# Gated cross block on one core: h of the last tiles turned by a transposing DMA instead of by TensorE

## The chip, the core and the metric

The kernel runs on one core of a Trainium2 chip. A core has four compute engines, each with its own instruction stream: TensorE (PE, matrix products and transposes into PSUM), VectorE (DVE), ScalarE (ACT) and GpSimd (POOL), and a fifth, SyncE (SP), which here only issues DMA transfers. They are kept in step by semaphores. The metric is the device time of one execution in microseconds (us), and the median of several runs is compared.

## The reference

The inputs are x (4 x 512 x 512), a context (4 x 512 x 256), two gates and weights. A selective scan (Mamba) over the context gives a branch that is gated by the layer-normed x and added to x; then a feed-forward block with quantised activations and ternary weights is added. Only the second half matters to this change:

```python
def _act_quant(x):
    scale = 127.0 / jnp.clip(jnp.max(jnp.abs(x), axis=-1, keepdims=True), EPS)
    return jnp.round(jnp.clip(x * scale, -128.0, 127.0)) / scale      # forward value
def _bitlinear(x, w):
    return jnp.einsum('bsi,oi->bso', _act_quant(_rmsnorm(x)), _weight_quant(w))
gate = jax.nn.silu(_bitlinear(x, w_gate))          # 512 -> 2048
up = _bitlinear(x, w_up)                           # 512 -> 2048
return _bitlinear(gate * up, w_down)               # h = gate * up, 2048 -> 512
x = x + tanh(g_xattn) * mamba(ctx, layernorm(x));  x = x + tanh(g_ffn) * ffn(layernorm(x))
```

## The kernel before, in words

The 2048 rows of x (4 batches of 512) are 16 tiles of 128 rows. The scan half works in 16 units s of 128 channels, and from unit 4 on the feed-forward part of tile s - 4 runs between the instructions of unit s. After the last unit (s = 15) the feed-forward parts of tiles 12 to 15 are left, with the end of tile 11 and the down projection of tile 10. This last stretch, from about 550 us on, is where the change acts.

What a tile t needs there, with the names and lines of the code:

- `xq_late` / `xq_transpose` (L546): four TensorE transposes of the quantised x, copied by ScalarE to `xqT` (`copy_xqT`, L1052).
- `late_gate` and `late_up` (L552): for each of four chunks c of 512 columns, four matmuls for gate and four for up.
- `gate_silu` (L1060, ScalarE) and `times_up` (L1406, VectorE) make one chunk of h, 128 x 512 floats. h of a tile is 128 x 2048.
- `squares` (L1066, ScalarE), `h_max` (L1410, VectorE), `h_rstd` (L831, GpSimd, 128 x 1) and `h_scales` (L1419 to L1424, VectorE) give the quantising factor.
- `scale_h` (L1088, ScalarE), twice, each half of h: times the factor, plus MAGIC = 1.5 * 2^23, which rounds to an integer.
- `hq_transpose` (L583, TensorE): 16 transposes of 128 x 128, four into each of four PSUM fillings, in two groups of eight; `copy_hqT` (L1093, ScalarE), four times, each taking MAGIC off and writing bf16 to `hqT`.
- `down` (L596, TensorE): 16 matmuls with the ternary down weights into `pT`; `output` (L1430, VectorE) scales it, adds x, and `store` (L322, SP) writes it out.

Each engine's order is written out by hand. In the tail's iteration of tile t TensorE does gate and up of chunk 0, then the down projection of tile t - 2, then gate and up of chunks 1, 2 and 3, with the x transposes of tile t + 1 and the h transposes of tile t - 1 among them. ScalarE does four Silus, with `scale_h(t - 1, 0)` behind the second and `scale_h(t - 1, 1)` behind the third. In the iteration of tile 15 both scalings stand ahead of the second Silu. `down(t - 2)` for t = 13, 14, 15 belongs to tiles 11, 12, 13, and the down of tile 14 stands at the end of the iteration of tile 15. Tile 15 itself is quantised in quarters by VectorE (L1555) and transposed and projected in quarters (L769, L1279, L620). `hqT`, `xqT`, `xn` and `o_buf` have two buffers each, as has h in the tail (`h_main`, `h_late`).

## Time and profile before

| | us |
|---|---|
| median of 3 runs | 621.03 (620.51 to 621.07) |
| span of the profiled execution, first to last instruction | 617.3 |
| PE busy | 520.0 (84%) |
| DVE busy | 557.0 (90%) |
| ACT busy | 519.0 (84%) |
| POOL busy | 508.1 (82%) |

For the profiled execution itself only the span is given, no whole time; the span lies 3.7 us under the median of the runs. The shares are means over the whole program. In the page's 40 slices POOL is at 9 tenths until slice 35 and at 3, 1, 0, 0, 0 after it, PE at 9, 8, 9, 9, 9, 6 in the last six. So a change in the tail is to be read in rows of the tail. The granted clock of TensorE (PEclk) is 0.9 or more there; 1.00 is 2.4 GHz and 0.50 is 1.2 GHz.

### The profile page before, as it was taken

The page shows a single profiled execution, that of the slowest core. Times are in us where ns is not written, and L with a number is a line of the kernel's source. Part 1 is how long each engine was busy: PE and PEld are TensorE (multiplying, and loading weights), DVE is VectorE, ACT ScalarE, POOL GpSimd, SP SyncE. Part 2 cuts the span into 40 slices and gives each one's busy share as a digit, 9 for nine tenths or more (in the row PEclk, how much of TensorE's full clock was granted, in tenths as well). Part 3 has the DMA queues.
Part 4 walks back from the last instruction along what each step waited for, and adds up shares of the span by engine and source line. Part 5 has one row for each costly group of instructions (what it writes and reads, how often), then busy time and mean ns, then how long its engine had stood idle before and what let it go on. Part 6 is the DMA issues. An engine that isn't in the chain of part 4 may idle for free. (4 is left out here: it accounts for less than half of the span.)

```text
span 617.3 us, 9751 instructions
## 1 busy us (share of the span) xinstructions
PE 520.0 (84%) x3254; PEld 363.1 (59%) x3254; DVE 557.0 (90%) x766; ACT 519.0 (84%) x796; POOL 508.1 (82%) x286
## 2 busy tenths in 40 slices
PE   6999666757776888999879989998799898999996
PEld 2443355646664767676747666666467666655553
DVE  2899979999999899999899999998999999987564
ACT  4869788985998899899798999997988988768884
POOL 2568799999999899999999999999999999931000
PEclk9999768989699999999999999999999999999999
DMA  9992941620751010117501111175111110000001
GB/s 286 401 414 88 354 156 34 245 80 1 271 206 52 0 53 2 35 35 277 188 31 35 36 35 35 35 266 195 35 35 36 35 36 18 2 18 18 18 19 51
DMA packets 30420, 64.25 MB, mean 104 GB/s; under 512 B 3729, under 2 KB 11921, under 8 KB 27554
## 3 DMA queue, kind: packets, MB, share of 16 engines
q1 hardware_dynamic: 30370, 63.63, 29.1%
q8 instruction: 26, 0.43, 0.3%
q14 instruction: 24, 0.20, 0.1%
HBM read 55.49 MB, written 8.13 MB: 103 GB/s over the span
## 5 line engine op out<-in xcount | busy, mean ns | idle before, releaser
L850 POOL TENSOR_TENSOR area_s<-area_s,b_bc 128x1024 f32<-128x1024 f32 x117 | 275.0, 2363 | 13.8 <-DVE u_all L1454 9.2
L483 PE MATMUL pY<-ident,area_s 128*128 128x128 f32 x532 | 87.6, 290 | 56.6 <-DVE area_s L1462 56.6
L552 PE MATMUL pG<-wq_gu,area_f 128*128 128x512 fp8e4 x448 | 107.9, 379 | 4.0 <-ACT area_f L1052 2.9
L1454 DVE TENSOR_TENSOR_SCAN area_s<-pA,area_s 128x512 f32<-128x512 f32 x88 | 105.2, 1207 | 5.1 <-ACT pA L1107 4.4
L483 PEld LDWEIGHTS pY<-ident,area_s 128*128 128x128 f32 x532 | 61.6, 146 | 78.0 <-DVE area_s L1462 70.5
L1107 ACT ACTIVATE pA<-dt_all,a_neg 128x512 f32<-128x512 f32 x145 | 97.7, 682 | 10.7 <-DVE area_s L1454 5.9
L842 POOL TENSOR_TENSOR u_all<-u_all 128x1024 f32<-128x1024 f32 x44 | 103.9, 2361 | 0.2 <-DMA u_all<-bc_rows 0.2
L1462 DVE TENSOR_TENSOR area_s<-area_s,pC 128x512 f32<-128x512 f32 x133 | 87.9, 664 | 0.8 <-DVE area_s L1454 0.5
L477 PE MATMUL pC<-ident,xdT 128*128 128x128 f32 x532 | 83.2, 283 | 3.6 <-DVE area_s L1462 2.3
L477 PEld LDWEIGHTS pC<-ident,xdT 128*128 128x128 f32 x532 | 64.3, 143 | 8.9 <-DVE area_s L1462 7.4
L552 PEld LDWEIGHTS pG<-wq_gu,area_f 128*128 128x128 bf16 x448 | 41.7, 98 | 47.1 <-ACT area_f L1052 3.9
L596 PE MATMUL pT<-wq_dn,area_f 128*128 128x512 fp8e4 x240 | 57.5, 379 | 0.0
L483 PE MATMUL pY<-ident,u_all 128*128 128x128 f32 x352 | 48.7, 284 | 2.0 <-POOL u_all L842 2.0
L831 POOL TENSOR_TENSOR sm<-sm,neg_half 128x1 f32<-128x1 f32 x16 | 8.8, 552 | 44.9 <-ACT sm L1070 33.7
L483 PEld LDWEIGHTS pY<-ident,u_all 128*128 128x128 f32 x352 | 42.2, 147 | 5.3 <-POOL u_all L842 2.4
L1406 DVE TENSOR_TENSOR area_f<-area_f,pG 128x512 f32<-128x512 f32 x52 | 34.6, 678 | 8.3 <-PE pG L552 6.3
L1107 ACT ACTIVATE pC<-dt_all,a_neg 128x512 f32<-128x512 f32 x57 | 38.9, 683 | 3.4 <-DVE u_all L1454 2.4
L1454 DVE TENSOR_TENSOR_SCAN u_all<-pA,area_s 128x512 f32<-128x512 f32 x33 | 39.6, 1212 | 0.1
L1060 ACT ACTIVATE area_f<-pG,sm 128x512 f32<-128x512 f32 x52 | 34.4, 685 | 4.3 <-PE pG L552 3.3
L583 PE MATMUL pG<-ident,area_f 128*128 128x128 f32 x176 | 24.0, 278 | 15.9 <-ACT area_f L1093 13.1
L795 POOL TENSOR_TENSOR area_s<-area_s 128x511 f32<-128x511 f32 x16 | 20.0, 1269 | 20.0 <-DVE area_s L1293 20.0
L1454 DVE TENSOR_TENSOR_SCAN area_s<-pC,area_s 128x512 f32<-128x512 f32 x29 | 35.0, 1207 | 1.4 <-ACT pC L1107 1.4
(211 smaller groups left out, 1143.9 us busy)
## 6 DMA issues: line engine op xcount, KB each, us to landing
b_bc<-bc_rows SPq DMA_DIRECT2D x14, 1024.0 KB, 6.5
area_s<-x SPq DMA_DIRECT2D x32, 256.0 KB, 2.9
u_all<-bc_rows SPq DMA_DIRECT2D x14, 512.0 KB, 5.9
b_bc<-w_gate SPq DMA_DIRECT2D x1, 4096.0 KB, 14.5
dt_all<-x SPq DMA_DIRECT2D x1, 4096.0 KB, 24.8
area_f<-w_up SPq DMA_DIRECT2D x1, 4096.0 KB, 34.2
area_f<-w_down SPq DMA_DIRECT2D x1, 4096.0 KB, 14.4
out<-area_f SPq DMA_DIRECT2D x16, 256.0 KB, 2.1
```

Of the source, the lines that this page charges most:

```text
L477: mm = pe.transpose(c_bank(s, m)[:, k * P:(k + 1) * P], xdT[:, s // NT, k, NS + n:NS + n + 1].to_broadcast([P, P]), ident[:, :])
L483: mm = pe.matmul(pY[:, k * P:(k + 1) * P], src[:, k * P:(k + 1) * P], ident[:, :], is_transpose=True, start=(first and k == 0), stop=(last ...
L552: mm = pe.matmul(bank, xqT[t % 2][:, k, :], wq_gu[:, k, m, c * GW:(c + 1) * GW], start=(k == 0), stop=(k == NT - 1))
L583: mm = pe.transpose(banks[r % 2][:, k * P:(k + 1) * P], h_of(t)[:, (4 * r + k) * P:(4 * r + k + 1) * P], ident[:, :])
L596: mm = pe.matmul(pT[:, :], hqT[t % 2][:, k, :], wq_dn[:, k, :], start=(k == 0), stop=(k == FK - 1))
L842: gp.tensor_tensor(hp[j], hp[j], c_bc[j], ALU.mult).then_inc(S["s_pmul"], 1)
L850: gp.tensor_tensor(db[c % NDB], du[s % 2].rearrange("p (a l) -> p a l", a=1).to_broadcast([P, CH, L]), b_bc[:, CH * c:CH * c + CH, :], ALU ...
L1060: act.activation(h_of(t)[:, c * GW:(c + 1) * GW], bank, ACT.Silu, scale=col(CS[t % 2])).then_inc(S["f_silu"], 1)
L1107: act.activation(exp_bank(s, n), dt_all[:, s, :], ACT.Exp, scale=a_neg[:, s % NT, n:n + 1]).then_inc(S["s_exp"], 1)
L1406: dve.tensor_tensor(chunk, chunk, bank, ALU.mult).then_inc(S["f_h"], 1)
L1454: dve.tensor_tensor_scan(h, at, dbu, 0.0, ALU.mult, ALU.add).then_inc(S["s_scan"], 1)
L1462: dve.tensor_tensor(p_st[i % NH], h_st[i % NH], c_bank(s, m), ALU.mult).then_inc(S["s_mul"], 1)
```

## The change

For tiles 11 to 14 (`DMA_FROM` = 11) `hq_transpose` and `copy_hqT` are gone. In their place GpSimd takes MAGIC off each half of the scaled h and writes bf16 into `hb`, two new views of 128 x 2048 bf16 in space of `u_all` that the scan no longer uses (`h_whole`, semaphore `f_hb`); then SP issues one transposing DMA from `hb` to `hqT` (`turn_h`, semaphore `f_hqD`); then `down` waits for `f_hqD`. A Silu that writes over an h buffer now waits for GpSimd's passes of the tile before last, where it waited for TensorE's transposes. Tile 15 is done as before. The stores of tiles 11, 12 and 13 stand behind the next tile's `turn_h` on SP.

```diff
--- before.py
+++ after.py
@@ -42,6 +42,8 @@
 DPARTS = -(-FK // DK)
 HR = FK // 4
 
+DMA_FROM = UNITS - NT - 1
+
 
 def pooled(s):
 
@@ -108,7 +110,7 @@
     d_xz0 d_xz1 d_xr0 d_xr1 d_bbc0 d_bbc1 d_bbc2 d_bbc3 d_c0 d_c1 d_c2 d_c3 d_u0 d_u1 d_out0 d_out1
     s_exp s_dbu s_scan s_mul s_pmul s_pytr s_cb s_ytr s_du s_skip s_skd s_dup s_duT s_diag s_dbp s_amul s_aytr d_ca s_sz s_szp s_szT s_y s_x1
     f_bn f_sum f_dev f_ve f_rr f_xn f_xs f_e f_xm f_xqp f_xqT f_gate f_silu f_up f_h f_sq f_mh f_rh f_hs f_hm
-    f_hqp f_hqT f_dn f_o e_y e_x1 e_sq e_max e_ss""".split()
+    f_hqp f_hqT f_hb f_hqD f_dn f_o e_y e_x1 e_sq e_max e_ss""".split()
 
 
 def past(eng, sem, value):
@@ -213,6 +215,8 @@
 
         z_buf = [zn, zt]
 
+        hb = [u_all[:, 2 + 2 * i:4 + 2 * i, :].rearrange("p n l -> p (n l)").bitcast(BF16) for i in range(2)]
+
         pA = ps("pA", [P, 2, 512])
         pC = ps("pC", [P, 2, 512])
         pY = ps("pY", [P, 512])
@@ -386,8 +390,21 @@
                     load_c_alone(s // NT)
                 if s >= 7:
                     store(s - 7)
-            for t in range(UNITS - 7, UNITS):
-                store(t)
+            def turn_h(t):
+
+                past(sp, S["f_dn"], t - 1)
+                past(sp, S["f_hqD"], 16 * (t - DMA_FROM))
+                sp.wait_ge(S["f_hb"], 2 * (t - DMA_FROM) + 2)
+                sp.dma_start_transpose(hqT[t % 2], hb[t % 2]).then_inc(S["f_hqD"], 16)
+
+            store(UNITS - 7)
+            store(UNITS - 6)
+            for t in range(DMA_FROM, UNITS - 1):
+                turn_h(t)
+                if t > DMA_FROM:
+                    store(t - 1)
+            store(UNITS - 2)
+            store(UNITS - 1)
             sp.wait_ge(S["d_out0"], 16 * UNITS // 2)
             sp.wait_ge(S["d_out1"], 16 * UNITS // 2)
 
@@ -585,7 +602,10 @@
 
             def down(t, part, z_done):
                 if part == 0:
-                    pe.wait_ge(S["f_hqT"], HR * t + HR)
+                    if t < DMA_FROM:
+                        pe.wait_ge(S["f_hqT"], HR * t + HR)
+                    else:
+                        pe.wait_ge(S["f_hqD"], 16 * (t - DMA_FROM) + 16)
                     past(pe, S["f_o"], t)
 
                     if z_done < UNITS:
@@ -615,7 +635,7 @@
                         keep_on(s)
 
             def down_quarter(t, r):
-                pe.wait_ge(S["f_hqT"], HR * t + r + 1)
+                pe.wait_ge(S["f_hqT"], HR * DMA_FROM + r + 1)
                 for k in range(4 * r, 4 * r + 4):
                     mm = pe.matmul(pY[:, :], hqT[t % 2][:, k, :], wq_dn[:, k, :], start=(k == 0), stop=(k == FK - 1))
                 return mm
@@ -723,7 +743,6 @@
             y_sum(s, 14)
             y_sum(s, 15)
             up(t - 1, 3)
-            pC_banks = (pC[:, 0, :], pC[:, 1, :])
 
             def xq_late(t):
                 past(pe, S["f_xqT"], t)
@@ -744,9 +763,6 @@
                     late_up(t, c)
                     if c == FC - 1:
                         xq_late(t + 1)
-                    if c >= 2:
-                        hq_transpose(t - 1, 2 * c - 4, pC_banks)
-                        hq_transpose(t - 1, 2 * c - 3, pC_banks)
             t = UNITS - 1
             late_gate(t, 0)
             late_up(t, 0)
@@ -755,16 +771,11 @@
             for c in range(1, FC):
                 late_gate(t, c)
                 late_up(t, c)
-                if c < 3:
-                    hq_transpose(t - 1, 2 * c - 2, pC_banks)
-                    hq_transpose(t - 1, 2 * c - 1, pC_banks)
             for part in range(DPARTS):
                 down(t - 1, part, UNITS)
 
             for r in range(HR):
                 pe.wait_ge(S["f_hm"], 2 * t + r + 1)
-                if r < 2:
-                    pe.wait_ge(S["f_hqT"], HR * t - 1 + r)
                 for k in range(4):
                     mm = pe.transpose(end_bank(r)[:, k * P:(k + 1) * P], h_of(t)[:, (4 * r + k) * P:(4 * r + k + 1) * P], ident[:, :])
                 mm.then_inc(S["f_hqp"], 1)
@@ -917,12 +928,21 @@
 
             gp.wait_ge(S["s_y"], UNITS)
             gp.tensor_tensor(dt_all[:, UNITS - 1, P:], szT[:, P:], xr[(UNITS - 1) % 2][:, P:], ALU.add).then_inc(S["s_x1"], 1)
-            h_rstd(t - 1)
-            x_rstd(t + 1)
-            for t in range(UNITS - NT + 1, UNITS + 1):
+
+            def h_whole(t):
+
+                past(gp, S["f_hqD"], 16 * (t - DMA_FROM - 1))
+                for i in range(2):
+                    gp.wait_ge(S["f_hm"], 2 * t + i + 1)
+                    half = h_of(t)[:, i * F // 2:(i + 1) * F // 2]
+                    gp.tensor_scalar(hb[t % 2][:, i * F // 2:(i + 1) * F // 2], half, -MAGIC, 1.0, ALU.add, ALU.mult).then_inc(S["f_hb"], 1)
+
+            for t in range(UNITS - NT, UNITS):
                 h_rstd(t - 1)
                 if t + 1 < UNITS:
                     x_rstd(t + 1)
+                h_whole(t - 1)
+            h_rstd(UNITS - 1)
 
         @block.scalar
         def _(act):
@@ -1056,7 +1076,10 @@
                     act.wait_ge(S["k_p3"], 3 * NW)
                 act.wait_ge(S["f_xs"], 5 * t + 5)
                 act.wait_ge(S["f_gate"], FC * t + c + 1)
-                past(act, S["f_hqp"], HR * (t - (1 if t < UNITS - NT else 2)) + HR)
+                if t <= UNITS - NT:
+                    past(act, S["f_hqp"], HR * (t - (1 if t < UNITS - NT else 2)) + HR)
+                else:
+                    act.wait_ge(S["f_hb"], 2 * (t - 2 - DMA_FROM) + 2)
                 act.activation(h_of(t)[:, c * GW:(c + 1) * GW], bank, ACT.Silu, scale=col(CS[t % 2])).then_inc(S["f_silu"], 1)
 
             def squares(t):
@@ -1224,7 +1247,6 @@
                     if n == 15 and s + 1 < UNITS:
                         copy_duT(s + 1)
 
-            pC_banks = (pC[:, 0, :], pC[:, 1, :])
             t = UNITS - NT
 
             part_squares(t - 1, 0, 3, 0)
@@ -1248,24 +1270,16 @@
                 scale_h(t - 1, 0)
                 gate_silu(t, 2, late_bank(2, 0))
                 scale_h(t - 1, 1)
-                copy_hqT(t - 1, 0, pC_banks)
-                copy_hqT(t - 1, 1, pC_banks)
                 scale_x(t + 1)
                 gate_silu(t, 3, late_bank(3, 0))
                 copy_xqT(t + 1, pY[:, :])
-                copy_hqT(t - 1, 2, pC_banks)
-                copy_hqT(t - 1, 3, pC_banks)
             t = UNITS - 1
             squares(t - 1)
             gate_silu(t, 0, late_bank(0, 0))
             scale_h(t - 1, 0)
             scale_h(t - 1, 1)
             gate_silu(t, 1, late_bank(1, 0))
-            copy_hqT(t - 1, 0, pC_banks)
-            copy_hqT(t - 1, 1, pC_banks)
             gate_silu(t, 2, late_bank(2, 0))
-            copy_hqT(t - 1, 2, pC_banks)
-            copy_hqT(t - 1, 3, pC_banks)
             part_squares(t, 0, 2, 0)
             gate_silu(t, 3, late_bank(3, 0))
             act.wait_ge(S["f_e"], t + 1)
@@ -1275,7 +1289,7 @@
             part_squares(t, 3, 4, 2)
             add_squares(PSS, PSS + 2, SS, 5, 2, "f_sq")
             for r in range(HR):
-                act.wait_ge(S["f_hqp"], HR * t + r + 1)
+                act.wait_ge(S["f_hqp"], HR * DMA_FROM + r + 1)
                 act.activation(hqT[t % 2][:, 4 * r:4 * r + 4, :], end_bank(r).rearrange("p (k t) -> p k t", t=P),
                                ACT.Copy, bias=-MAGIC).then_inc(S["f_hqT"], 1)
 
```

TensorE, in the iteration of tile 13, from behind the down projection of tile 11 to that of tile 12. `pG`, `pA` are banks for gate and up, `pC` for the transposed h, `pY` for the transposed x, `pT` for the down projection; `area_f`, `area_s` hold h, `hqT` and `xqT`. Before:

```order
L552 MATMUL pA<-wq_gu,area_f 128x512 x8
L552 MATMUL pG<-wq_gu,area_f 128x512 x8
L583 MATMUL pC<-ident,area_s 128x128 x8
L552 MATMUL pA<-wq_gu,area_f 128x512 x8
L546 MATMUL pY<-ident,area_f 128x128 x4
L583 MATMUL pC<-ident,area_s 128x128 x8
L552 MATMUL pG<-wq_gu,area_f 128x512 x8
L596 MATMUL pT<-wq_dn,area_f 128x512 x16
```

And in the changed kernel, the same stretch (from the second chunk of tile 13 to the first of tile 14):

```order
L569 MATMUL pA<-wq_gu,area_f 128x512 x8
L569 MATMUL pG<-wq_gu,area_f 128x512 x8
L569 MATMUL pA<-wq_gu,area_f 128x512 x8
L563 MATMUL pY<-ident,area_f 128x128 x4
L569 MATMUL pG<-wq_gu,area_f 128x512 x8
L616 MATMUL pT<-wq_dn,area_f 128x512 x16
```

Both groups of eight h transposes are gone, and the x transposes are followed by the next tile's gate at once.

ScalarE, the iteration of tile 13. `L1060` (after: L1083) is the Silu, `L1088` (L1111) the scaling of half of h, `L1093` the copy of the transposed h, `L1045` (L1065) the scaling of x, `L1052` (L1072) the copy of the transposed x. Before:

```order
L1060 ACTIVATE area_f<-pA,sm 128x512
L1088 ACTIVATE area_s<-area_s,sm 128x1024
L1060 ACTIVATE area_f<-pG,sm 128x512
L1088 ACTIVATE area_s<-area_s,sm 128x1024
L1093 ACTIVATE area_f<-pC 128x512 x2
L1045 ACTIVATE area_f<-area_f,sm 128x512
L1047 ACTIVATE sm<-sm,k_prod 128x1
L1060 ACTIVATE area_f<-pA,sm 128x512
L1052 ACTIVATE area_f<-pY 128x512
L1093 ACTIVATE area_f<-pC 128x512 x2
```

In the changed kernel:

```order
L1083 ACTIVATE area_f<-pA,sm 128x512
L1111 ACTIVATE area_s<-area_s,sm 128x1024
L1083 ACTIVATE area_f<-pG,sm 128x512
L1111 ACTIVATE area_s<-area_s,sm 128x1024
L1065 ACTIVATE area_f<-area_f,sm 128x512
L1067 ACTIVATE sm<-sm,k_prod 128x1
L1083 ACTIVATE area_f<-pA,sm 128x512
L1072 ACTIVATE area_f<-pY 128x512
```

The scalings keep their place between the Silus; the four copies are gone.

GpSimd and SP at the end of the changed kernel, first GpSimd (`L842` and `L836` are the 128 x 1 powers that were there before):

```order
L842 TENSOR_TENSOR sm<-sm,neg_half 128x1
L836 TENSOR_TENSOR sm<-sm,neg_half 128x1
L938 TENSOR_SCALAR u_all<-area_s 128x1024 x2
L842 TENSOR_TENSOR sm<-sm,neg_half 128x1
L836 TENSOR_TENSOR sm<-sm,neg_half 128x1
L938 TENSOR_SCALAR u_all<-area_f 128x1024 x2
```

Two passes a tile are new, behind both powers. On SP:

```order
L326 DMA out<-area_f 128x512 x3
L398 DMA_TRANSPOSE area_f<-u_all 128x16x128 x2
L326 DMA out<-area_f 128x512
L398 DMA_TRANSPOSE area_f<-u_all 128x16x128
L326 DMA out<-area_f 128x512
L398 DMA_TRANSPOSE area_f<-u_all 128x16x128
L326 DMA out<-area_f 128x512 x3
```

Before, eight stores stood here in a row; now four transposing DMAs stand among them.

## Rows read from the trace of the kernel before

**Rows 1.** Windows, one tail period: window, its length, busy of PE, PEld, DVE, ACT, POOL, PEclk, DMA, GB/s.
```profile
571.00:584.00 13.00, 12.93 (x71) 6.90 (x70) 8.47 (x18) 10.73 (x17) 1.06 (x2) 1.00 0.06 21
```

**Rows 2.** Chain of waits, 567 to 584 us: start, length, what.
```profile
567.62 3.45 PE pT L596 x16
...
574.53 0.87 PE pC L583 x8
...
577.20 0.63 PE pY L546 x4
577.83 0.87 PE pC L583 x8
578.70 1.73 PE pG L552 x8
580.43 3.45 PE pT L596 x16
```

**Rows 3.** Timeline of ScalarE, 561 to 579 us: start, length, instruction, idle before.
```profile
561.52 1.15 ACT L1088 ACTIVATE area_f<-area_f,sm 128x1024 f32<-128x1024 f32 x1
...
572.02 0.69 ACT L1060 ACTIVATE area_f<-pA,sm 128x512 f32<-128x512 f32 x1 [2.00 <-issue]
...
574.34 1.14 ACT L1088 ACTIVATE area_s<-area_s,sm 128x1024 f32<-128x1024 f32 x1
575.38 1.07 ACT L1093 ACTIVATE area_f<-pC 128x512 bf16<-128x512 f32 x2
576.33 0.73 ACT L1045 ACTIVATE area_f<-area_f,sm 128x512 f32<-128x512 f32 x1
...
577.87 0.60 ACT L1052 ACTIVATE area_f<-pY 128x512 bf16<-128x512 f32 x1
```

**Rows 4.** Timelines of ScalarE, VectorE and TensorE, the last tile.
```profile
596.43 2.19 ACT L1088 ACTIVATE area_s<-area_s,sm 128x1024 f32<-128x1024 f32 x2 [1.39 <-DVE sm L1423]
603.50 0.69 ACT L1060 ACTIVATE area_f<-pA,sm 128x512 f32<-128x512 f32 x1
604.29 0.69 DVE L1406 TENSOR_TENSOR area_f<-area_f,pA 128x512 f32<-128x512 f32 x1 [1.17 <-ACT area_f L1060]
603.46 3.62 PE L596 MATMUL pT<-wq_dn,area_f 128*128 128x512 fp8e4 x16
608.15 1.09 PE L769 MATMUL pC<-ident,area_f 128*128 128x128 f32 x8 [1.07 <-DVE area_f L1555]
```

**Rows 5.** Groups of GpSimd by form: count, busy us, mean ns, idle before.
```profile
L842 POOL TENSOR_TENSOR u_all<-u_all 128x1024 f32<-128x1024 f32 x44 | 103.9, 2361 | 0.2 <-DMA u_all<-bc_rows 0.2
...
L805 POOL TENSOR_SCALAR b_bc<-b_bc 128x2048 f32<-128x2048 f32 x1 | 1.9, 1893 | 0.1
```

**Rows 6.** DMA issues by line, KB, median us to landing; L293 also min/median/max.
```profile
u_all<-bc_rows SPq DMA_DIRECT2D x14, 512.0 KB, 5.9
out<-area_f SPq DMA_DIRECT2D x16, 256.0 KB, 2.1
b_bc<-bc_rows SPq DMA_DIRECT2D x2, 512.0 KB, 7.4
u_rows<-u_all SPq DMA_DIRECT2D x1, 512.0 KB, 20.1
DMA to landing us min/median/max: 3.7/5.9/12.3
```

**Rows 7.** TensorE idle in the scan part: timeline rows, then windows as in Rows 1.
```profile
134.23 0.66 PE L483 MATMUL pY<-ident,area_s 128*128 128x128 f32 x4 [2.41 <-DVE area_s L1462]
135.94 1.12 PE L483 MATMUL pY<-ident,area_s 128*128 128x128 f32 x4 [1.06 <-DVE area_s L1462]
191.92 0.66 PE L483 MATMUL pY<-ident,area_s 128*128 128x128 f32 x4 [3.50 <-DVE area_s L1462]
136.00:138.00 2.00, 2.00 (x10) 2.00 (x11) 2.00 (x2) 2.00 (x4) 2.00 (x2) 0.50 0.00 0
190.00:192.00 2.00, 0.08 (x1) 0.09 (x2) 2.00 (x5) 2.00 (x6) 2.00 (x2) 1.00 0.00 0
```

## The prediction, made before the changed kernel ran

> **What bounds the kernel now.** I read the windows first, then the chain of waits, then the timeline of each engine, all for the stretch after the last scan. From about 556 us on only the feed-forward part of tiles 12 to 15 is left. TensorE fills that stretch: in 571 to 584 us it is busy 12.93 of 13 us at clock 1.00, ScalarE 10.73, VectorE 8.47, GpSimd 1.06 [rows 1]. The chain of waits says the same: it runs through PE piece after piece [rows 2]. The reader is to see one tile in it: down projection of tile 11 from 567.62, of tile 12 from 580.43, so a period of 12.81 us = 4 x 1.73 (gate and up) + 3.45 (down) + 2 x 0.87 (the sixteen transposes of h) + 0.07 + 0.63 (transposes of x). So in the tail TensorE is the bound, and the edited pieces stand on its path. The third thing to read is the other engines' side of the loop, because the change puts GpSimd and a transfer into it: ScalarE's order in one tile [rows 3], and the last tile, whose end does not follow TensorE alone [rows 4].
>
> **What is removed.** Per tile two pieces of 0.87 us on TensorE and two of 1.07 on ScalarE. They are not worth the same.
>
> The first piece (574.53) stands between matmuls that wait for nothing: 0.87 us is gained. The second (577.83) stands between the x transposes and the next tile's gate, and that gate needs ScalarE's copy of those transposes, 577.87 to 578.47 [rows 3]. Without the second piece the gate starts at about 578.5 where the chain has it at 578.70 (its first matmul overlaps the last transposes, so less than the 0.2 is real): I take 0.05. The x transposes themselves can move up by the 0.87: they wait for the scaling of x (576.33 to 577.06), and the h copies before it on ScalarE (575.38, 1.07) go too, which puts its end at about 576.1, before TensorE arrives at 577.20 - 0.87 = 576.33. So 0.92 us for each of the iterations of tiles 12, 13 and 14: 2.8 us. In the iteration of tile 15 there are no x transposes, so both pieces count: 1.74. At the very end the down projection of tile 14 (from 603.46, 3.45 long) is done at about 607, but the next transposes start at 608.15, released by VectorE; that wait is fed by ScalarE's last Silu at 603.50, VectorE's product at 604.29 and then the squares [rows 4]. Silu stood behind two h copies and half the squares; with the copies gone it can start as soon as its gate matmuls are done, about 0.65 us before TensorE's last up matmul instead of at it. I take 0.65 for that. Together 2.8 + 1.74 + 0.65 = 5.2 us if nothing new is waited for. ScalarE's freed 2.14 us a tile is otherwise slack.
>
> **What is added.** Two GpSimd passes over 128x1024 (float to bf16), a transposing DMA of 128x2048 bf16 = 512 KB, and a wait of the down projection for it in place of one for ScalarE's copies. GpSimd is free (1.06 of 13 us busy). The nearest row for a pass is its one-input operation over 128x2048, 1893 ns [rows 5], half of it with a little overhead 1.05 us; from above the two-input 128x1024 operation, 2361 ns; from below half of 1893, 0.95. I take 1.05. The first half overlaps ScalarE's scaling of the second, so only one pass is in line. The new wait of the Silu for the h buffer (GpSimd's passes of the tile two back) falls due about 2 us after they end: nothing.
>
> On SP the transposing DMA of a tile waits for GpSimd's passes, and the store of the tile before stands behind it. That store's data come from the down projection one iteration later, so neither holds the other; the DMA of tile 11 stands behind the store of tile 10, whose sum VectorE writes at about 557 us, 6 us too early to matter.
>
> **The loop.** Call Z the time from issue to landing of one such DMA. Down of tile 11 ends at 571.07. Behind it come gate 1 and its Silu (572.02), the first scaling, gate 2's Silu, and the second scaling, which ends at 574.34 + 1.14 = 575.48 [rows 2, 3]: 4.41 us after down's end. Plus 1.05 for GpSimd and 0.06 for two semaphores, the DMA is issued 5.52 us after the end of the previous down. TensorE would come to the next down 12.81 - 0.92 - 3.45 = 8.44 us after it. So TensorE stands still for Z - 2.92 at each down. For the first (tile 11) the second scaling ends at 561.52 + 1.15 = 562.67, the DMA is issued at 563.78, TensorE arrives at 567.62 - 0.92 = 566.70: again Z - 2.92. This is a loop: a stalled down delays gate 1, so the Silu, so both scalings of the next tile, so the next DMA. It is not caught up. It holds for the downs of tiles 11, 12 and 13. The down of tile 14 is different: its scalings stand ahead of tile 15's second Silu, so they do not wait for down 13. On the old clock they end at 596.43 + 2.19 = 598.62 [rows 4], less about 0.7 because the squares ahead of them stood behind two h copies; plus 1.11 the DMA is issued at 599.0 and lands at 599.0 + Z. TensorE arrives at 603.46 - 1.74 + (Z - 2.92) = 598.8 + Z. So it is about 0.2 us late, inside the roughly 0.6 us of slack that the end still has (1.07 of waiting at 608.15 [rows 4], less what the earlier Silu uses up). Sum: 3 x (Z - 2.92) - 5.2 = 3Z - 14.0, and -5.2 at the least. Break-even is Z = 4.65 us.
>
> **What Z is.** No row shows a transposing DMA. By bytes the nearest are the 512 KB transfers into SBUF: median 5.9 us over 14, with a least of 3.7 and a most of 12.3; 7.4 us for two others; and 20.1 for one 512 KB store in the crowded start. A store of 256 KB in the quiet tail takes 2.1 [rows 6]. From below that 2.1 us, at which nothing stalls. From above 12.3, beyond it 20.1. The destination is written in 256-byte runs (a row of hqT holds 16 blocks of 128 bf16), shorter than those of any of these rows, and these transfers partly queue behind each other, which pulls the other way. I take a value between the two medians for 512 KB, 6.6 us. The sum is then 3 x 6.6 - 14.0 = +5.8 us. TensorE would stand 3.7 us at each of three downs.
>
> The Trainium skill speaks against that value. Its page "Advanced Engine Details and Errata", section X-Bar Transpose (TRN2), says that transposing DMAs on this chip are as fast as ordinary ones, 350 to 400 GB/s. No run here shows one yet. By that rule the 512 KB would land like the fastest ordinary one, and the change would be a gain. Its page "VectorE: DVE Perf Modes", section The three transpose paths, gives 1309 ns for one 128x128 block by DMA against 390 ns on TensorE; sixteen such blocks one behind the other would be 20.9 us, an estimate by that page, and the sum +49 us.
>
> **From the profiled execution to the result.** The profiled span is 617.3 us; the median of the timed runs is 621.03, 3.7 us more, which I keep. 617.3 + 5.8 = 623.1 us of span, 626.9 us as time.
>
> **Rivals.**
> 1. The transfer is hidden or nearly so. Mechanism: the DMA lands as quickly as the fastest 512 KB row (3.7), since SP's queue and the DMA engines are nearly idle in the tail (share 0.06 [rows 1]). Then each down waits 0.8 us and the sum is 3 x 3.7 - 14.0 = -2.9: 618.1 us; below 2.92 us it is -5.2: 615.8. It decides from Z below 4.2 us. For it: the quiet queue. Against it: the short runs, and that half of these rows took 5.9 or more. The Trainium skill's rule on the crossbar, above, is this rival.
> 2. The gain and the wait cancel, Z from 4.2 to 5.1: 620 to 622 us. A measurement of this kernel can't tell under 0.2% (1.24 us) from no change.
> 3. Turning is the limit, not the bytes: Z from 9.4 us up. At 12.3 the sum is 3 x 12.3 - 14.0 = +22.9: 643.9 us; at the 20.1 of the crowded store it would be +46.3. For it: short runs, 512 KB written as 2048 runs of 256 bytes. Against: no row of a quiet stretch takes that long.
> 4. The stalls also cost TensorE's clock. After standing 2.41 and 1.06 us with four matmuls between, the granted clock was 0.50 (1.2 GHz), and four transposes took 1.12 us in place of 0.66; but after standing 3.50 us in one piece behind dense work it was still 1.00, and they took 0.66 [rows 7]. With stalls of 3.7 us behind dense matmuls the second case is the nearer, so I count nothing. If it does fall and each of the three downs runs at half clock, that is 3 x 3.45 = 10.4 more: 637.3 us.
>
> That the change does not do what it says I exclude: the sixteen transposes and four copies a tile are gone from the order, and the transposing DMA stands there once a tile.
>
> **How the numbers follow.** Forecast (Z between 5.1 and 9.4 at full clock, 622.3 to 635.3) 42%, rival 1 22%, rival 2 7%, rival 3 20%, rival 4 9%. That gives faster 22%, same 7%, slower 71%. The likeliest is the forecast at 626.9. The range that leaves out 2 in 10: from Z = 3.5 (-3.5: 617.5) to Z = 12.3 (644).
>
> **What would show it.** In the changed profile: the DMA issue row of the transpose with its time to landing, 6.6 us; waits of the down matmuls on that DMA, three of about 3.7 us and a fourth under 1; the period from down to down 3.45 + 5.52 + 6.6 = 15.6 us in place of 12.81; GpSimd's passes of about 1.05; the gate after the x transposes starting right at the end of ScalarE's copy; ScalarE's last Silu ahead of the end of the up matmuls; clock 1.00 throughout. The prediction is wrong in size if Z is off (3 us of time for each us of Z), and wrong in kind if a stall of one down does not delay the next DMA, or if the down of tile 14 waits as long as the others.

## The result, and the profile after

| | before | changed |
|---|---|---|
| median of 20 runs each | 620.61 us (618.95 to 621.54) | 623.2 us (619.16 to 626.52) |
| ratio | | 1.0039, 95% interval 1.0026 to 1.0053 |
| span of the profiled execution | 617.3 us | 621.2 us |
| start of the down projection of tile 10 in it | 550.64 us | 552.13 us |
| from there to the end of the span | 66.7 us | 69.1 us |

The change makes the kernel slower by 0.39%, 2.4 us by the ratio. The forecast was 5.8 us slower. The loop that the prediction named is there, but the size is off by more than a factor of two, and the direction came out right only because errors in the sum cancelled, as the part on the prediction shows. 1.5 us of the 3.9 us between the two spans arise before the tail and are not the change's, as a second profile of the kernel before will show. So the rows below are compared from the down projection of tile 10 on.

Timeline of TensorE in the changed kernel, the rows of the down projection (L616) and the gates ahead of it (L569): start, length, instruction, idle time before it and what ended it. They answer to [rows 2].

```profile
566.23 1.90 PE L569 MATMUL pG<-wq_gu,area_f 128*128 128x512 fp8e4 x8 [0.69 <-ACT area_f L1072]
569.76 3.63 PE L616 MATMUL pT<-wq_dn,area_f 128*128 128x512 fp8e4 x16 [1.63 <-DMA area_f<-u_all]
...
579.86 1.90 PE L569 MATMUL pG<-wq_gu,area_f 128*128 128x512 fp8e4 x8 [0.69 <-ACT area_f L1072]
583.36 3.63 PE L616 MATMUL pT<-wq_dn,area_f 128*128 128x512 fp8e4 x16 [1.60 <-DMA area_f<-u_all]
...
597.56 5.31 PE L616 MATMUL pT<-wq_dn,area_f 128*128 128x512 fp8e4 x16 [2.20 <-DMA area_f<-u_all]
...
608.53 3.61 PE L616 MATMUL pT<-wq_dn,area_f 128*128 128x512 fp8e4 x16 [0.48 <-issue]
```

Three downs wait for the DMA, 1.63, 1.60 and 2.20 us, where 3.7 each was forecast; from down to down it is 13.60 us, where 15.6 was forecast. The fourth has 0.48 us of idle time that is not put down to the DMA. It is VectorE's: the sum of tile 13, which reads the same PSUM bank, stands behind the maxima of tile 15 and ends at 608.43, and the down may overwrite the bank only then (0.10 us later it starts):

```profile
607.09 0.69 DVE L1428 TENSOR_REDUCE sm<-area_f 128x1 f32<-128x512 f32 x1
607.69 0.74 DVE L1444 SCALAR_TENSOR_TENSOR area_f<-pT,sm,dt_all 128x512 f32<-128x512 f32 x1
```

The third down is also long, 5.31 us where the others take 3.6. The windows say why (columns as in [rows 1]):

```profile
596.00:598.00 2.00, 0.44 (x2) 0.21 (x3) 1.34 (x6) 0.60 (x2) 0.54 (x1) 0.96 0.88 246
598.00:600.00 2.00, 2.00 (x6) 0.75 (x5) 0.56 (x1) 2.00 (x2) 0.81 (x1) 0.50 0.00 0
600.00:602.00 2.00, 2.00 (x8) 0.76 (x7) 0.00 (x0) 0.07 (x1) 1.24 (x2) 0.68 0.00 0
602.00:604.00 2.00, 2.00 (x11) 0.88 (x9) 0.00 (x0) 0.17 (x1) 0.00 (x0) 1.00 0.82 156
```

After standing still for 2.20 us TensorE was granted 0.50 (1.2 GHz) for some 3 us, which cost 5.31 - 3.62 = 1.69 us.

The loop itself is in the chain of waits of the changed kernel (start, length, what), one turn of it:

```profile
573.38 1.73 PE pA L569 x8
575.11 0.88 PE pG L569 x4
...
576.14 1.04 POOL u_all L938
577.18 0.64 issue
...
577.87 1.05 POOL u_all L938
...
579.00 4.32 DMA area_f<-u_all
583.32 0.05 issue
583.36 3.63 PE pT L616 x16
```

TensorE's gates, GpSimd's passes, the DMA and the down follow one another (ScalarE's second scaling runs beside the first pass and in the 0.64 us of "issue"). In [rows 2] this chain held PE pieces alone. The DMA takes 4.32 us from issue to landing. Of all four:

```profile
L398 SPq DMA_TRANSPOSE area_f<-u_all x4: 1652/1854/3133, 565.4 to 601.3; - x4
...
DMA to landing us min/median/max: 4.3/4.3/4.9
```

The tail adds up. What a wait costs is read from starts, since the idle time shown is some 0.15 us short (the ends of matmuls are modelled). From the last gate to the down it is 569.76 - 566.23 = 3.53 us, then 3.50 and 4.10. Where nobody waits it is 1.74, as an experiment below shows. So the three waits cost 1.79 + 1.76 + 2.36 = +5.9, and the slow down +1.7. With the -5.2 forecast for the removed work that is +2.4 us, and 69.1 - 66.7 is 2.4.

### The profile page after: what moved, and what is told of

It is laid out like the page before. It is cut to its first block and busy times, and to the rows that moved or that the text cites. A ratio compares the mean times of both kernels' runs of the same rounds, so it can differ in the third digit from the quotient of the medians.

```text
span 621.2 us, 9591 instructions
## 1 busy us (share of the span) xinstructions
PE 521.2 (84%) x3190; PEld 360.8 (58%) x3190; DVE 556.7 (90%) x766; ACT 512.0 (82%) x780; POOL 516.5 (83%) x294
## 5 line engine op out<-in xcount | busy, mean ns | idle before, releaser
L500 PE MATMUL pY<-ident,area_s 128*128 128x128 f32 x532 | 89.3, 294 | 52.6 <-DVE area_s L1476 52.6
L569 PE MATMUL pG<-wq_gu,area_f 128*128 128x512 fp8e4 x448 | 108.0, 379 | 6.0 <-ACT area_f L1072 5.0
L500 PEld LDWEIGHTS pY<-ident,area_s 128*128 128x128 f32 x532 | 63.0, 148 | 74.1 <-DVE area_s L1476 66.5
L494 PE MATMUL pC<-ident,xdT 128*128 128x128 f32 x532 | 85.1, 288 | 3.6 <-DVE area_s L1476 2.3
L494 PEld LDWEIGHTS pC<-ident,xdT 128*128 128x128 f32 x532 | 66.0, 146 | 8.9 <-DVE area_s L1476 7.4
L569 PEld LDWEIGHTS pG<-wq_gu,area_f 128*128 128x128 bf16 x448 | 41.7, 98 | 50.0 <-ACT area_f L1072 6.6
L616 PE MATMUL pT<-wq_dn,area_f 128*128 128x512 fp8e4 x240 | 59.2, 388 | 5.9 <-DMA area_f<-u_all 5.4
L616 PEld LDWEIGHTS pT<-wq_dn,area_f 128*128 128x128 bf16 x240 | 23.6, 100 | 29.7 <-DMA area_f<-u_all 6.9
L1083 ACT ACTIVATE area_f<-pG,sm 128x512 f32<-128x512 f32 x52 | 34.4, 684 | 5.3 <-PE pG L569 4.3
L806 POOL TENSOR_TENSOR area_s<-area_s 128x511 f32<-128x511 f32 x16 | 20.0, 1270 | 20.9 <-DVE area_s L1307 20.9
```

The costliest lines, as they stand in the source:

```text
L494: mm = pe.transpose(c_bank(s, m)[:, k * P:(k + 1) * P], xdT[:, s // NT, k, NS + n:NS + n + 1].to_broadcast([P, P]), ident[:, :])
L500: mm = pe.matmul(pY[:, k * P:(k + 1) * P], src[:, k * P:(k + 1) * P], ident[:, :], is_transpose=True, start=(first and k == 0), stop=(last ...
L569: mm = pe.matmul(bank, xqT[t % 2][:, k, :], wq_gu[:, k, m, c * GW:(c + 1) * GW], start=(k == 0), stop=(k == NT - 1))
L616: mm = pe.matmul(pT[:, :], hqT[t % 2][:, k, :], wq_dn[:, k, :], start=(k == 0), stop=(k == FK - 1))
L1083: act.activation(h_of(t)[:, c * GW:(c + 1) * GW], bank, ACT.Silu, scale=col(CS[t % 2])).then_inc(S["f_silu"], 1)
```

## The experiments

"Tail" is the time from the start of the down projection of tile 10 to the end of the span in the profiled execution: the one number that the part before can't disturb.

| kernel | time, us | before on the same chip | ratio (95%) | down of tile 10 starts | tail |
|---|---|---|---|---|---|
| before, first profile | 620.61 | | | 550.64 | 66.7 |
| before again | 620.82 (1 run) | 620.44 | | 552.31 | 66.7 |
| changed | 623.2 | 620.61 | 1.0039 (1.0026 to 1.0053) | 552.13 | 69.1 |
| changed again | 621.55 | 620.0 | 1.0025 (1.001 to 1.004) | 551.71 | 67.3 |
| nobody waits for the DMA | 614.91 | 620.0 | 0.9914 (0.9898 to 0.993) | 552.52 | 61.5 |
| DMA in two halves | 615.24 | 620.0 | 0.9929 (0.9902 to 0.9955) | 550.98 | 62.0 |
| TensorE kept busy | 622.6 | 620.0 | 1.0041 (1.0029 to 1.0054) | 552.44 | 68.3 |
| down one chunk later | 616.5 | 620.44 | 0.9931 (0.9909 to 0.9952) | 552.95 | 62.6 |
| halves, and down later | 615.76 | 620.44 | 0.9931 (0.9917 to 0.9945) | 552.30 | 61.4 |
| DMA twice | 640.47 | 620.44 | 1.0331 (1.0302 to 1.036) | 550.56 | 85.5 |
| ordinary copy, runs of 4 KB | 617.13 | 620.34 | 0.9952 (0.9935 to 0.9969) | 551.19 | 63.0 |
| ordinary copy, runs of 240 bytes | 620.98 | 620.34 | 1.0024 (1.0005 to 1.0042) | 550.04 | 66.4 |

**Nobody waits for the DMA.** The down reads `hb`, h before it is turned. The rest stays: passes, DMAs, matmuls. GpSimd, ScalarE and SP get waits of their own (for the down and for landings), so that no buffer is written while it is still read.

```diff
-                        pe.wait_ge(S["f_hqD"], 16 * (t - DMA_FROM) + 16)
+                        pe.wait_ge(S["f_hb"], 2 * (t - DMA_FROM) + 2)
...
-                    mm = pe.matmul(pT[:, :], hqT[t % 2][:, k, :], wq_dn[:, k, :], ...
+                    mm = pe.matmul(pT[:, :], left[:, k, :], wq_dn[:, k, :], ...   # left: hb[t % 2] for t >= 11
```

> The down projection of tiles 11 to 14 reads hb (h before it is turned) as soon as GpSimd has written it, so its product is not the reference's; all DMAs, passes and matmuls remain, only nobody waits for the transposing DMA. Theory (what the change takes off is worth 5.2 us, and all that it gives back is the wait for the DMA and what that wait does to TensorE's clock): the three waits of 1.6, 1.6 and 2.2 us, the 0.48 and the slow down of tile 13 all go, time 5.2 us under the kernel before, 615.4, clock 1.00 in the tail. Rival (the transposing DMA or GpSimd's passes disturb the other engines, or the program is slower before its tail): the tail gains less than 4 us or the part before 550 us is over 1 us later, time 617 or more.

Measured: 614.91 us. The tail is 66.7 - 61.5 = 5.2 us shorter. TensorE waits for no DMA there (what was waited for, us in total, times, longest):

```profile
PE pG L570 <- ACT area_f L1075: 2.8, 4, 0.7
PE pY L564 <- ACT area_f L1068: 0.8, 1, 0.8
PE pT L618 <- issue: 0.5, 1, 0.5
PE pY L642 <- ACT area_f L1298: 0.3, 1, 0.3
```

So the sum of what is removed was forecast right to 0.1 us, and all that the change gives back comes from the wait. By the tail, GpSimd's passes and the DMA traffic cost nothing measurable. The 0.48 us ahead of the down of tile 14 ("issue") is here too, although that down waits for no DMA: it is VectorE's sum, as above, and a part of the 5.2, not of what is given back.

**The DMA in two halves.**

```diff
-                sp.wait_ge(S["f_hb"], 2 * (t - DMA_FROM) + 2)
-                sp.dma_start_transpose(hqT[t % 2], hb[t % 2]).then_inc(S["f_hqD"], 16)
+                for i, name in enumerate(("f_hqD", "f_hqE")):
+                    past(sp, S[name], 16 * (t - DMA_FROM))
+                    sp.wait_ge(S["f_hb"], 2 * (t - DMA_FROM) + i + 1)
+                    sp.dma_start_transpose(hqT[t % 2][:, FK // 2 * i:FK // 2 * (i + 1), :], hb[t % 2][:, F // 2 * i:F // 2 * (i + 1)]).then_inc(S[name], 16)
...
+                    if k == FK // 2 and t >= DMA_FROM:                 # in down
+                        pe.wait_ge(S["f_hqE"], 16 * (t - DMA_FROM) + 16)
```

> The transposing DMA in two halves of 256 KB, each issued as soon as GpSimd has written its half, and the down projection waits for the second only before its ninth matmul. Theory (the wait is for this DMA's 4.3 us and is in the loop): the first half is issued 1.7 us earlier and is there before TensorE arrives, the second lands within the first eight matmuls; all stalls go if a half lands in 3.5 us or less: 615.4 to 616.5. Rival (landing is a fixed cost that does not fall with size, and two DMAs behind each other on the queue take longer than one): the second half lands 5 us or more after issue, the ninth matmul waits 0.5 to 1 us, time 617 to 619.

Measured: 615.24 us. A half lands in 3.1 us in the median, and one of eight in 4.8:

```profile
L399 SPq DMA_TRANSPOSE area_f<-u_all x8: 1231/1240/1347, 562.5 to 596.9; - x8
...
DMA to landing us min/median/max: 3.1/3.1/4.8
```

The only wait left is 0.42 us, for that late one, ahead of the ninth matmul of the down of tile 13. The rival falls: landing does depend on size, 3.1 us for 256 KB and 4.3 for 512 KB. As an estimate from these two sizes alone that is 1.2 us for each 256 KB over some 1.9 that stay; the two halves of a tile are issued 1.3 to 1.7 us apart and so overlap.

**TensorE kept busy ahead of the wait.**

```diff
+                        if t < UNITS - 2:
+                            for k in range(8):
+                                pe.transpose(pC[:, k // 4, k % 4 * P:(k % 4 + 1) * P], ident[:, :], ident[:, :])
                         pe.wait_ge(S["f_hqD"], 16 * (t - DMA_FROM) + 16)
```

> Eight transposes of the identity into a PSUM bank that nobody reads, ahead of the wait of the downs of tiles 11, 12 and 13, so that TensorE stands still 0.7 to 1.3 us there in place of 1.6 to 2.2. Theory (the fall of TensorE's clock behind a stall costs some runs 1.7 us a time, and makes the spread of 619 to 626 us): 1 to 3 us faster than the changed kernel, near 621.3, spread under 3 us, clock 1.00 in the tail. Rival (the spread and the rest come from the DMA's own landing time, 4.3 to 4.9 us): no faster than the changed kernel, 623, same spread.

Measured: 622.6 us, five runs within 622.51 to 622.99. The clock is 1.00 in every window from 566 to 608 us, the three downs take 3.63 us each, and the spread is 0.5 us where the changed kernel has 7.4. But the time is not lower, as the theory wanted, so it was half borne out. The second wait shows why:

```profile
570.06 3.63 PE L619 MATMUL pT<-wq_dn,area_f 128*128 128x512 fp8e4 x16 [0.75 <-DMA area_f<-u_all]
...
585.16 3.63 PE L619 MATMUL pT<-wq_dn,area_f 128*128 128x512 fp8e4 x16 [2.23 <-DMA area_f<-u_all]
...
598.77 3.63 PE L619 MATMUL pT<-wq_dn,area_f 128*128 128x512 fp8e4 x16 [0.74 <-DMA area_f<-u_all]
```

The second DMA took 5.82 us to land, the others 4.3. Since a wait here is worth its full length, that one transfer costs 1.5 us, and without it the time would be 621.1, near the theory's 621.3 (an estimate). So this run does not tell how much of the changed kernel's median is the clock's. It tells that the length of a stall does not decide alone: behind the eight transposes 2.23 us of standing still left the clock at 1.00, where 2.20 us in the changed kernel brought it to 0.50.

**The changed kernel again.**

> The changed kernel again, for a second profile and its time on the same chip as the others. Theory (the loss is the stalls, 5.9 us against a gain of 5.2, plus a clock that falls in some of them): about 623, spread again over 4 us, and the part before 550 us within 0.5 us of the kernel before in a mean over profiles. Rival (the part before the tail is 1.5 us slower, as in the first profile): the down of tile 10 again starts 1.5 us later than in the kernel before.

Measured: 621.55 us over 12 runs, 1.4 under the theory, spread 618.95 to 624.0. Waits of 1.64, 1.61, 2.08 and 0.48; this time all downs take 3.6 us. By starts the three waits cost 1.79, 1.77 and 2.24 us. The tail is 67.3: -5.2 + 5.8 = +0.6 over before. The down of tile 10 starts at 551.71, 1.1 us later than in the first profile of the kernel before, which leaves the rival to the next run. The same kernel thus has a tail of 67.3 or 69.1 us, and 1.7 of the 1.8 us between them is the one down at a lower clock.

**The kernel before again.**

> The kernel before, once more, for a second profile. Theory (the part before the tail is the same in both kernels, and the first profile of the kernel before was an early one): the down projection of tile 10 starts at 551 to 552.5 us, as in the profiles of the changed kernels (550.98 to 552.52), and from there to the end it takes 66.7 us again. Rival (the change slows the scan part by 1 to 1.5 us): it starts at 550.6 again.

Measured: the down of tile 10 starts at 552.31 us, with a tail of 66.7 again. The two profiles of one and the same kernel differ by 1.7 us before the tail, as much as those of the changed kernels and their variants (550.04 to 552.95). The rival falls: the change does nothing there that these profiles show.

**Down one chunk later** (tiles 11 to 13; the same edit in the iteration of tile 15).

```diff
-                if t > UNITS - NT:
-                    for part in range(DPARTS):
-                        down(t - 2, part, UNITS)
                 for c in range(1, FC):
                     late_gate(t, c)
                     late_up(t, c)
+                    if c == 1 and t > UNITS - NT:
+                        for part in range(DPARTS):
+                            down(t - 2, part, UNITS)
```

> The changed kernel with the down projection of tiles 11, 12 and 13 put behind the second chunk's gate and up instead of the first's. Theory (the wait is a loop: down, gate 1, Silu, two scalings, GpSimd, DMA, next down; with down behind chunk 1 it no longer holds up the Silu that stands ahead of the scalings): the three waits go although the DMA still takes 4.3 us; the down of tile 14 then waits about 1.2 us; 616.0. Rival (TensorE waits as long wherever down stands, because the DMA is slow, not because of the loop): the waits shrink by no more than the 1.73 us of the chunk moved ahead of them and the Silus come later, 618 to 620.

Measured: 616.5 us.

```profile
570.58 3.63 PE L616 MATMUL pT<-wq_dn,area_f 128*128 128x512 fp8e4 x16
...
582.46 3.63 PE L616 MATMUL pT<-wq_dn,area_f 128*128 128x512 fp8e4 x16
...
594.89 3.63 PE L616 MATMUL pT<-wq_dn,area_f 128*128 128x512 fp8e4 x16 [0.43 <-DMA area_f<-u_all]
...
603.01 3.63 PE L616 MATMUL pT<-wq_dn,area_f 128*128 128x512 fp8e4 x16 [1.04 <-DMA area_f<-u_all]
```

With the same DMA, still 4.3 us in the median, the first two waits are gone. The third is 0.43, because that DMA took 4.87 us, and the down of tile 14, which was not moved, waits 1.04 because its TensorE work now arrives earlier. All but the 0.43 was forecast.

The reason that the theory gave is only half of it. The down no longer stands ahead of chunk 1, but it still stands ahead of chunk 2, and the Silu of chunk 2 stands ahead of the second scaling. ScalarE, behind the down that starts at 570.58, and SP:

```profile
575.16 0.69 ACT L1084 ACTIVATE area_f<-pG,sm 128x512 f32<-128x512 f32 x1 [2.34 <-PE pG L569]
575.75 1.14 ACT L1112 ACTIVATE area_s<-area_s,sm 128x1024 f32<-128x1024 f32 x1
```

```profile
578.10 1.70 SPq L398 DMA_TRANSPOSE area_f<-u_all  x1
```

So the loop is not opened but made shorter by one chunk. The DMA of tile 12 is issued at 578.10, 7.5 us after the start of the down of tile 11 (9.24 in the changed kernel), and lands 4.31 later: 11.8 us, what TensorE's own work takes from down to down (11.83 where nobody waits). The waits shrank by 1.72 us, which the rival allowed too (up to 1.73); what speaks against the rival is the time. And there is no slack: 0.5 us of lateness in the third DMA came through as 0.5 us of wait.

**Both.**

> Both: the transposing DMA in two halves, and the downs of tiles 11 to 13 behind the second chunk. Theory: no wait for a DMA is left, not even where one lands 0.5 to 1.5 us late, so the time of the kernel in which nobody waits for the DMA: 614.9, 5.2 us under the kernel before, spread as that of the kernel before. Rival (down behind chunk 1 makes the sums or the last tile late): 616 or more.

Measured: 615.76 us, 0.9 over the theory and under the rival's 616, the spread 615.25 to 616.97 (1.7 us; the kernel before has 2.3 on that chip). Tail 61.4, where the kernel in which nobody waits has 61.5. No wait for a DMA is left in it. This is the version to keep of those run. Its ratio to before, 0.9931, is that of the halves alone (0.9929), so its gain over them is not shown by the times.

**The DMA twice**, the second after the first has landed.

```diff
-                sp.dma_start_transpose(hqT[t % 2], hb[t % 2]).then_inc(S["f_hqD"], 16)
+                sp.dma_start_transpose(hqT[t % 2], hb[t % 2]).then_inc(S["f_hqE"], 16)
+                sp.wait_ge(S["f_hqE"], 16 * (t - DMA_FROM) + 16)
+                sp.dma_start_transpose(hqT[t % 2], hb[t % 2]).then_inc(S["f_hqD"], 16)
```

> Each transposing DMA is issued twice, the second when the first has landed, and the down projection waits for the second. Theory (loop: each us of landing time costs 3 us, three times, and the down of tile 14 nearly nothing more): the time from issue to landing rises by 4.4 us, the three waits by 4.4 each, 13.2 us over the changed kernel, 635, and up to 1.7 us more for each down at a lower clock, 635 to 640. Rival (the wait is caught up by the next tile, since the second wait starts later): 4.4 to 6 us over the changed kernel, 626 to 628.

Measured: 640.47 us (638.26 to 643.83), just over the 635 to 640 of the theory.

```profile
572.47 5.19 PE L618 MATMUL pT<-wq_dn,area_f 128*128 128x512 fp8e4 x16 [5.92 <-DMA area_f<-u_all]
...
591.87 5.72 PE L618 MATMUL pT<-wq_dn,area_f 128*128 128x512 fp8e4 x16 [5.84 <-DMA area_f<-u_all]
...
611.86 5.96 PE L618 MATMUL pT<-wq_dn,area_f 128*128 128x512 fp8e4 x16 [5.89 <-DMA area_f<-u_all]
...
623.48 3.61 PE L618 MATMUL pT<-wq_dn,area_f 128*128 128x512 fp8e4 x16 [0.48 <-issue]
```

Each of the three waits grows by about 4.3 us (5.92 - 1.64, 5.84 - 1.61), by 3.8 for the third, whose DMA had been late in the changed kernel; the fourth not at all. That is 12.3 us for the waits, and 6.0 for downs at a lower clock (5.19 + 5.72 + 5.96 - 3 x 3.63): 18.3, and the tail is 85.5 - 67.3 = 18.2 longer. The rival, that a wait is caught up, would have given 4.4 to 6. The loop shows in the issues too: from the first DMA of one tile to that of the next it is 19.5 and 19.9 us here, 13.6 in the changed kernel and 11.8 where nobody waits.

**An ordinary copy in place of the transposing one**, once in long runs and once in short ones; h is then not turned. (The semaphore at the end of each line is left out here.)

```diff
-                sp.dma_start_transpose(hqT[t % 2], hb[t % 2])
+                sp.dma_start(hqT[t % 2].rearrange("p k t -> p (k t)"), hb[t % 2])                                  # long
+                sp.dma_start(hqT[t % 2][:, :, 0:120], hb[t % 2].rearrange("p (k t) -> p k t", t=P)[:, :, 0:120])   # short
```

> An ordinary DMA of the same 512 KB from hb to hqT in runs of 4 KB, in place of the transposing one, so h is not turned; everything waits as in the changed kernel. Theory (the transposing DMA is held by its 2048 short pieces, not by the transposing or by a fixed cost): it lands in 3.0 to 3.7 us, at 3.3 us the three waits are 0.6 us, 617.0. Rival (any 512 KB from SBUF to SBUF takes this long in the tail): 4.3 us to landing, waits of 1.6 us, 621 to 623.

> The same ordinary DMA, but of the first 120 of every 128 bf16, so in 2048 runs of 240 bytes, 480 KB. h is not turned. Theory (short pieces set the time): 4.0 to 4.6 us to landing like the transposing DMA, waits of 1.3 to 1.9 us, 621 to 623. Rival (transposing itself costs the time, short runs do not): it lands like the copy in long runs, within 0.4 us of it, and the kernel takes as long as that one.

The issue rows of both, first the long, then the short, each from its own kernel:

```profile
area_f<-u_all SPq DMA_DIRECT2D x4, 512.0 KB, 2.9
```

```profile
area_f<-u_all SPq DMA_DIRECT2D x4, 480.0 KB, 4.2
```

It is 2.9 us for 512 KB in runs of 4 KB, 4.2 for 480 KB in runs of 240 bytes, 4.3 for the transposing DMA. Between issue and landing the profile counts 144 packets for the long copy, 2064 for the short one and 2080 for the transposing DMA. So, with 32 KB less in the short copy, the short pieces cost at least 1.3 us and the transposing next to nothing. Both rivals fall. The waits follow: 0.25, 0.20 and 0.61 us at 617.13, and 1.49, 1.42 and 1.46 at 620.98. The profiled execution of the short copy is the fastest of its ten (618.69, the slowest 624.57), so its tail of 66.4, under that of the kernel before, says less than its median.

## Why the prediction was right or wrong

- **What is removed, 5.2 us.** Right in the sum, in part by luck. The kernel without the wait is 5.2 us shorter in its tail. By starts of the downs the iterations of tiles 12, 13 and 14 gain 1.0 each (0.92 forecast), that of tile 15 gains 1.1 (1.74 forecast, less VectorE's sum of tile 13), and the end 1.1 (0.65 forecast). That the second group of transposes is worth nothing is seen too: the gate waits 0.69 us for ScalarE's copy of the x transposes at each tile, where that group used to stand.
- **GpSimd's pass, 1.05 us.** Right: 1.04 and 1.05.
- **The loop.** Right in kind. The waits come three times, nearly alike, each us of landing time is paid three times (DMA twice), and a loop that is shorter by one chunk has just none left. The wait was forecast as Z - 2.92: with Z = 4.3 that is 1.4; by starts it is 1.8, so 1.1 us too little over the three. Of the difference 0.16 comes from mixing two views (from down's start to the end of the second scaling the timeline has 577.78 - 569.76 = 8.02 us, I had 3.45 + 4.41), 0.15 from hand-overs between engines, which are 0.21 us in the chain where I took 0.06, and 0.06 from TensorE's own round, 11.83 us and not 11.89.
- **The down of tile 14.** Right in effect: it adds nothing of the DMA's in the changed kernel, and 1.04 us once the three others are gone. But the DMA was not 0.2 us late: it landed at 605.59, 2.3 us before TensorE had done the last up, and 0.5 us before in the second profile. I had not seen that VectorE's sum of tile 13 would hold this down for 0.48 us.
- **What Z is, 6.6 us.** This is the step that failed. Measured 4.3, and 4.9 for the third. 3 x (6.6 - 4.3) = 6.9 us too much. By my own formula 4.3 gives 3 x 4.3 - 14.0 = -1.1: the true Z lies on the other side of my break-even of 4.65, in the band of rival 2 (4.2 to 5.1), and with it the formula has the changed kernel 1.1 us faster. Three things that the formula lacked bring the sum back: +0.6 for the late third transfer, +1.1 for the waits that were 0.4 us longer each than Z - 2.92, and +1.7 for the clock in one of two profiles. That is +2.3 with the clock and +0.6 without, as the tails have it (+2.4, +0.6). So the direction was right by luck. I took medians (5.9, 7.4), and they mix two kinds of load. Of the fourteen loads with the median of 5.9, four were issued at 289.41, 289.89, 295.03 and 300.89 us (each row from a short window of its own):

```profile
u_all<-bc_rows SPq DMA_DIRECT2D x1, 512.0 KB, 5.6
u_all<-bc_rows SPq DMA_DIRECT2D x1, 512.0 KB, 7.7
u_all<-bc_rows SPq DMA_DIRECT2D x1, 512.0 KB, 3.8
u_all<-bc_rows SPq DMA_DIRECT2D x1, 512.0 KB, 4.4
```

  The last two were issued 5 us and more behind the load before them; so were two of the last four, with 3.7 and 4.3. The tail has one such transfer at a time, and these four rows, 3.7 to 4.4, were the ones to read. That they come near 4.3 is in part chance: they load from DRAM and turn nothing, and a copy within SBUF in long runs took 2.9.
- **Bytes or runs.** I named the short runs as a reason for more time, and they are: 1.3 us. I weighed it with no number.
- **The Trainium skill on transposing DMAs.** What its page "Advanced Engine Details and Errata", section X-Bar Transpose (TRN2), says, that they are as fast as ordinary ones, holds here against an ordinary copy in runs as short (4.3 against 4.2 us), not against one in long runs (2.9). My estimate from the Trainium skill's page "VectorE: DVE Perf Modes", section The three transpose paths, sixteen times its 1309 ns or 20.9 us, was far off the 4.3 measured.
- **The clock, rival 4.** I had it as a case apart and at nothing in the forecast, because [rows 7] has a stall of 3.50 us behind dense work that left the clock at 1.00. Here 2.20 us, with 0.69 us of idle time 1.9 us ahead of it, was enough in one profile of the changed kernel and cost 1.7 us; in the other, with 2.08, the clock stayed. With stalls of 5.9 us all three downs ran slow. What decides below that is open.

So the net is small because a gain of 5.2 us was given back as 5.8 us of waiting for the DMA, and now and then 1.7 for the clock. What is not settled: by the tails the changed kernel is 0.6 to 2.4 us slower, by the medians 2.6 and 1.6; how often the clock falls would take many profiles. That this makes up its spread is argued from the busy version's 0.5 us over five runs, not counted; late transfers may have a part in it.

## What to carry to other kernels

Before a transfer is put in the place of engine work, follow the way round from its landing to its next issue: if that is a loop, every us of latency is paid once a turn, and the first question is not how long the transfer takes but which instruction ahead of its source waits for its reader. Moving the reader by one chunk, or issuing the transfer in halves, took a change from 0.4% slower to 0.7% faster. And price a transfer from rows of the same crowding and run length: a median over queued loads (5.4 to 7.9 us) is no price for a lone one (3.7 to 4.4).

## What the runs showed of the hardware that I had not expected

- A transposing DMA of 512 KB lands 4.3 us after issue, one of 256 KB in 3.1; an ordinary copy of 512 KB within SBUF in runs of 4 KB in 2.9, one of 480 KB in runs of 240 bytes in 4.2.
- SP's record for issuing it is long, 1.5 to 2.0 us for 512 KB (3.0 to 3.2 in three of the late ones below) and 1.24 for 256, against 0.47 and 0.60 for the two ordinary copies.
- Some transposing DMAs land late. Over all runs there are 44, and six took 4.8, 4.8, 4.9, 4.9, 5.6 and 5.8 us, the others 4.2 to 4.4 (3.1 to 3.3 for halves). In each of the six there is one packet of the queue that the profile calls q8, kind instruction (16 KB), between issue and landing. Of the 38 on-time ones 37 have none, and one has one. The DMA view first for the late one of the busy version (window 580 to 587 us), then for an on-time one, the second of the changed kernel (579 to 584), then for the exception, a half of the version with halves and down later (577.35 to 580.42):

```profile
q1 hardware_dynamic: 2224, 0.79, 49.9%
q8 instruction: 1, 0.02, 0.8%
issues: line engine op xcount, KB each, median us to landing
out<-area_f SPq DMA_DIRECT2D x1, 256.0 KB, 4.4
area_f<-u_all SPq DMA_TRANSPOSE x1, 5.8
```

```profile
q1 hardware_dynamic: 2224, 0.79, 69.4%
issues: line engine op xcount, KB each, median us to landing
out<-area_f SPq DMA_DIRECT2D x1, 256.0 KB, 3.1
area_f<-u_all SPq DMA_TRANSPOSE x1, 4.3
```

```profile
q1 hardware_dynamic: 1171, 0.50, 64.7%
q8 instruction: 1, 0.02, 3.2%
...
area_f<-u_all SPq DMA_TRANSPOSE x1, 3.1
```

  The late ones fit a fetch of instructions that holds back a part of the transfer, and the exception shows that such a packet need not delay it. That was seen, not tested: no run moved the fetch.
